# Expert tiles on GpSimd: the row store ahead of the next gather, the gather in the middle of the weight piece

## The reference

```python
x = x + tanh(g_xattn) * attention(layernorm(x), ctx, ctx, mask, W1, b1, W2, b2)
h = layernorm(x)
route = softmax(h @ router_w + router_b); e = argmax(route); p = max(route)
for each expert e:                       # w1[e]: 256 x 2048, w2[e]: 1024 x 256
    a, g = split(h @ w1[e], 2)
    y = (silu(a) * g) @ w2[e]            # kept for the tokens of e
x = x + tanh(g_ffn) * y * p
```

## Time and profile before

| | before |
|---|---|
| median of 3 runs | 448.74 us (445.57 to 452.37) |
| profiled execution, its own time | 449.49 us |
| its span, first to last instruction | 447.7 us |
| mean granted TensorE clock | 0.954 of 2.4 GHz |
| busy: PE, DVE, ACT, POOL | 401.3, 217.0, 176.5, 243.7 us |
| the loop over expert tiles | from about 107 us on |

### The profile page before, as it was taken

One profiled execution on the slowest core, in us unless ns is written; L12 is line 12 of the kernel. 1 busy time (PEld: TensorE's weight loads), 2 busy tenths in 40 slices (PEclk: granted clock), 3 DMA queues, 4 the chain that ended last, 5 costly groups with the idle time before them and its releaser, 6 DMA issues.

```text
span 447.7 us, 9834 instructions
## 1 busy us (share of the span) xinstructions
PE 401.3 (90%) x2431; PEld 346.5 (77%) x2432; DVE 217.0 (48%) x527; ACT 176.5 (39%) x338; POOL 243.7 (54%) x324
## 2 busy tenths in 40 slices
PE   5998984149989999999999999999999999999990
PEld 4787872027878888888888888888888888888880
DVE  4689899933454443444433444433444434444340
ACT  1167650024443454545532344445433543233230
POOL 2356997221865577887772258728852676232221
PEclk9999897559999999999999999999999999999996
DMA  7950233863333044333442003433331011000010
GB/s 204 360 199 2 95 107 131 85 175 108 118 118 117 23 166 163 135 117 116 134 155 83 27 17 117 134 112 124 117 117 35 4 35 35 24 24 27 24 33 12
DMA packets 29850, 44.01 MB, mean 98 GB/s; under 512 B 8377, under 2 KB 25581, under 8 KB 27791
## 3 DMA queue, kind: packets, MB, share of 16 engines
q1 hardware_dynamic: 24095, 34.45, 24.6%
q0 software_dynamic: 3456, 9.11, 6.3%
q10 hardware_dynamic: 2288, 0.33, 0.5%
HBM read 35.44 MB, written 8.83 MB: 99 GB/s over the span
## 4 chain that ended last, share of the span: by engine, by line
PE 80%; DVE 7%; POOL 6%; DMA 2%; issue 2%; ACT 1%; DVEq 0%; SPq 0%; POOLq 0%; ACTq 0%
PE py L1117 22%; PE pa L1099 21%; PE pg L1099 21%; PE ph L1109 7%; POOL w_lo L415 2%; PE px L1084 2%; DVE x_all L742 1%; PE ps_s L1024 1%; POOL rstd L399 1%; DMA ctx_in<-in_ctx 1%; DVE bn L750 1%; DMA x_sorted<-residual_rows,idx_gather 1%; PE ps_p L968 1%; PE ps_xt L940 1%; DVE x_norm L878 1%
## 5 line engine op out<-in xcount | busy, mean ns | idle before, releaser
L895 DVE TENSOR_TENSOR ht_lo<-ph,ht_hi 128x512 fp32r<-128x512 f32 x70 | 48.4, 691 | 135.4 <-ACT ht_hi L624 135.4
L493 POOL TENSOR_TENSOR w_lo<-staging,w_hi x84 | 107.1, 1304 | 7.3 <-ACT w_hi L645 4.0
L624 ACT CAST ht_hi<-ph 128x512 fp32r<-128x512 f32 x70 | 41.1, 586 | 118.6 <-PE ph L1109 83.4
L1117 PE MATMUL py<-w_hi,ht_hi 128*128 x280 | 81.3, 291 | 0.8 <-DVE out_tile L903 0.8
L1117 PE MATMUL py<-w_lo,ht_hi 128*128 x280 | 78.4, 280 | 0.0
L1117 PE MATMUL py<-w_hi,ht_lo 128*128 x280 | 78.3, 280 | 0.0
L482 POOL DMA_INDIRECT out<-out_tile,idx_now x34 | 34.6, 1019 | 72.6 <-DVE out_tile L903 72.0
L1099 PE MATMUL pa<-w_hi,xt_hi 128*128 (+1 forms) x140 | 58.7, 420 | 0.8 <-ACT xt_hi L606 0.8
L443 POOL DMA_INDIRECT x_sorted<-residual_rows,idx_now x34 | 35.6, 1048 | 39.5 <-DVE x_norm L878 21.4
L1099 PE MATMUL pg<-w_lo,xt_hi 128*128 (+1 forms) x140 | 55.9, 400 | 0.0
L1099 PE MATMUL pg<-w_hi,xt_hi 128*128 (+1 forms) x140 | 55.9, 399 | 0.0
(11 more groups left out here) (168 smaller groups left out, 583.2 us busy)
## 6 DMA issues: line engine op xcount, KB each, us to landing
staging<-in_L_ffn_w SPq DMA_DIRECT2D x24, 1024.0 KB
residual_rows<-x_all SPq DMA_DIRECT2D x8, 516.0 KB, 4.0
x_all<-in_x SPq DMA_DIRECT2D x8, 512.0 KB, 10.1
x_sorted<-residual_rows,idx_now POOLq DMA_INDIRECT x34
out<-out_tile,idx_now POOLq DMA_INDIRECT x34, 2.5
w_in<-in_L_xattn_W SPq DMA_DIRECT2D x2, 256.0 KB, 4.7
ctx_in<-in_ctx SPq DMA_DIRECT2D x1, 308.0 KB
mask_in<-in_fside_1xSxS ACTq DMA_DIRECT2D x1, 308.0 KB, 11.7
```

The lines of the kernel that those rows point to most:

```text
L493: lo = nc.gpsimd.tensor_tensor(out=w_lo[:, bass.ds(dst + q * QW, QW)], in0=staging[:, bass.ds(src + q * QW, QW)], in1=w_hi[:, bass.ds(dst ...
L624: nc.scalar.copy(ht_hi[:, j], ph[j][:]).then_inc(hhi_ready[j], 1)
L895: nc.vector.tensor_tensor(out=ht_lo[:, j], in0=ph[j][:], in1=ht_hi[:, j].bitcast(FP32), op=ALU.subtract).then_inc(hlo_ready[j], 1)
L1117: last = mm(py[:, 0:D], ht[:, j, c * P:(c + 1) * P], w[:, bass.ds(slot + (DC * PW + (j * HC + c) * D), D)], start=j == 0 and n == 0, stop= ...
```

## The change

In part 2 GpSimd's order within a tile becomes: load the piece number, index copies, store of tile t-1, quarters one and two of the weight piece, gather of tile t+2, quarters three and four. The piece's routine is cut into two halves, each in a branch of its own; in a tile without a piece both are skipped. The wait for `w_hi` stands ahead of the first half, the signal `w_ready` behind the last quarter, as before. The other engines' loops are not touched.

In part 1 the multiplication of round 0 by the token number moves from GpSimd to VectorE, where rounds 1 and 2 have it already, and the semaphore for it is gone.

```diff
-            end_group = ROUNDS[0][1]
-            pool.wait_ge(col_ready, 1)
-            nc.gpsimd.tensor_tensor(out=col_hot[:, 0:end_group], in0=col_hot[:, 0:end_group],
-                                    in1=token_of[:, 0:end_group].unsqueeze(2).to_broadcast([P, end_group, COLS, B]),
-                                    op=ALU.mult).then_inc(token_ready, 1)
...
-            def low_part(t):
-
-                piece = pool.value_load(tile_piece[:, bass.ds(t, 1)], min_val=0, max_val=E * PIECES - 1)
+            def low_half(piece, half):
+
                 with pool.If(piece > 0):
                     src = pool.snap((piece % PIECES) * PW)
                     dst = pool.snap(((piece // PIECES) & 1) * EW + src)
-                    pool.wait_ge(w_hi_ready, piece + (N_CHUNK - PIECES + 1))
-                    for q in range(QUARTERS):
+                    if half == 0:
+                        pool.wait_ge(w_hi_ready, piece + (N_CHUNK - PIECES + 1))
+                    for q in range(half * QUARTERS // 2, (half + 1) * QUARTERS // 2):
...
-                    lo.then_inc(w_ready, 1)
-
+                    if half == 1:
+                        lo.then_inc(w_ready, 1)
+
+            def piece_of(t):
+                return pool.value_load(tile_piece[:, bass.ds(t, 1)], min_val=0, max_val=E * PIECES - 1)
 
             def tile(t):
+                piece = piece_of(t)
                 index_copies(t)
+                scatter(t - 1, out_tile)
+                low_half(piece, 0)
                 pool.wait_ge(xnorm_ready, t + 2)
                 pool.wait_ge(res_ready, t + 2)
                 gather_rows(t + 2, idx_now[:, 0:1])
-                scatter(t - 1, out_tile)
-                low_part(t)
-
-            low_part(0)
+                low_half(piece, 1)
+
+            piece = piece_of(0)
+            low_half(piece, 0)
+            low_half(piece, 1)
             tile(1)
...
-                slots = nc.vector.tensor_tensor(out=slot_hot[:, at], in0=of_group(slot_iota, P),
-                                                in1=of_token(pos_f[:, 1], P), op=ALU.is_equal)
-                if r == 0:
-                    slots.then_inc(hot_ready, 1)
-                else:
-                    dve.wait_ge(col_ready, r + 1)
-                    nc.vector.tensor_tensor(out=col_hot[:, at], in0=col_hot[:, at], in1=of_token(token_v[:], COLS),
-                                            op=ALU.mult).then_inc(hot_ready, 1)
+                nc.vector.tensor_tensor(out=slot_hot[:, at], in0=of_group(slot_iota, P), in1=of_token(pos_f[:, 1], P),
+                                        op=ALU.is_equal)
+                dve.wait_ge(col_ready, r + 1)
+                nc.vector.tensor_tensor(out=col_hot[:, at], in0=col_hot[:, at], in1=of_token(token_v[:], COLS),
+                                        op=ALU.mult).then_inc(hot_ready, 1)
...
-                if r == 0:
-                    pe.wait_ge(token_ready, 1)
                 pe.wait_ge(hot_ready, r + 1)
```

More of the change, by code:

```diff
@@ L275, in flamingo_block @@
         col_ready = sem("col_ready")
-        token_ready = sem("token_ready")
         hot_ready = sem("hot_ready")
```

## The result

The changed kernel takes 561.86 us (median of 6 runs, 558.89 to 563.82), the kernel before in the same session 449.06 us (6 runs, 445.57 to 452.37): 1.250 times the time, 95% interval 1.246 to 1.254. The forecast was 546 us, so the loss is 113 us where 97 were forecast. The profiled execution of the changed kernel took 563.82 us.

A forecast was written before the change was run, and what follows sets the result against it. TensorE bounds the kernel before; after the change the ring does. Profiled 449.49 us + 71.4 for the loop - 0.6 for the sort = 520.3, with 26 for the clock 546 us; own range 528 to 575, wider range 512 to 576.

The forecast's parts named there:

- The ring: Expert loop, out_tile through store, half piece, gather and x_norm to out_tile: 12.91 us with a piece, 9.77 without.
- more in a tile that starts an expert: In six of 20 rings with a piece, the first quarter starts 1.43 and not 1.07 after the store: 2.2 us.
- The gather's setup: On GpSimd behind the second quarter: setup overlaps the running quarter, so the gather follows 0.05 us later; bounds 0 and 0.86.
- The lock on x_norm: VectorE's x_norm is held by GpSimd's quarters until 0.2 us after the fourth: 0.54 us per tile with a piece, 11 in all.
- the 0.15 us for the semaphore: Part of the 2.85 us taken for a gather travelling alone to land.
- The clock: TensorE idles 3.4 us in 20 tiles and falls to half clock in most: 1.3 us a tile, 26 us in all.
- the sort: Part 1, round 1: VectorE's indicator op shortens from 1.59 to 0.50 us; gain taken as 0.6 us.
- Full clock: Rival: late gather and all of the ring, but no clock falls in the loop; 520 us, chance 0.18.
- Setup not overlapping: Rival: gather's setup adds 0.81 us in each of 33 rings; 547 us at full clock, 573 with falls, chance 0.08.
- Gather beside a load: Rival: gather travels beside a weight load, 2.3 us more in 20 rings; 555 us without falls, 581 with, chance 0.05.
- Not slower: Rival: ring stays under TensorE's 9.52 us because rows reach x_norm in time; 447 us, chance 0.05.

The follow-up runs named there:

- warm kernel: Changed kernel plus 26 unread matmuls of 256 columns ahead of x_norm's transposes, in tiles whose predecessor carried a piece; 527.74 us, ratio 1.178.
- the kernel with the early load: Against the kernel before with only the multiplication moved to VectorE: piece number loaded at the tile's head, piece in one branch; 482.78 us, ratio 1.074.
- 13 matmuls: Changed kernel plus 13 unread matmuls of 256 columns ahead of x_norm's transposes, in tiles whose predecessor carried a piece; 534.8 us, ratio 1.191.
- the small copy: Changed kernel with the gather back ahead of the store, plus a 128x1 GpSimd copy between store and first quarter; 490.54 us, ratio 1.085.
- eight instructions: Changed kernel with the gather back ahead of the store, and the piece cut into eight instructions instead of four; 449.67 us, ratio 0.997.
- two halves: Changed kernel with the gather back ahead of the store, the two branches and the early piece-number load kept; 484.4 us, ratio 1.070.

## Why the prediction was right

**The ring** is the mechanism, as forecast. The length of it by steps, in the changed kernel against the prediction:

| step, in us | predicted | measured |
|---|---|---|
| out_tile's end to the store | 0.87 | 0.88 |
| store to first quarter, and two quarters | 3.62 | 3.61 |
| gap ahead of the gather, with a piece | 0.05 | 0.16 |
| gather's start to x_norm's end, with a piece | 3.85 | 3.72 |
| x_norm's end to out_tile's end, full clock | 4.52 | 4.50 |
| sum, with a piece | 12.91 | 12.87 |
| the same without a piece | 9.77 | 10.15 |
| more in a tile that starts an expert | 0.36 | 0.35 |
| x_norm's end to out_tile's end, more in a fall of the clock | 1.3 | 1.96 |

The store, the piece, the landing of the gather that travels alone, and the way back over px and `down` were all read off rows of the kernel before, and hold to 0.02 us but for the gather. One ring with a piece is 0.04 us shorter than forecast, which over 20 rings is 1 us. That it is so little is partly luck: the gap is 0.11 us longer than forecast, and gather's start to x_norm's end 0.13 shorter.

**The gather's setup** does overlap with the running quarters, so the rival with 0.81 us more in every ring fell: the gap is 0.16 us behind a quarter. Without a piece it is 0.31 us behind the store's record. The prediction had 0.04 there, as it let the gather follow after 1.07 like a quarter. These 13 rings took 132.0 us in place of 127.0: 3.5 us of it is that gap, the rest landings that came 0.3 to 0.8 us later in three of them. It is the second largest error.

**The lock on x_norm** holds: it ends 0.16 us behind the fourth quarter in 19 of 20 rings, and takes 0.72 us in the row above, not 0.41. It was worth less than the 0.54 us a tile taken for it. On the mean of the 20 rings x_norm starts 2.94 us after the gather's start (2.90 forecast; no row of the kernel before shows the 0.15 us for the semaphore in it) and takes 0.78, so the lock costs 0.37: the quarters end earlier than forecast, 3.56 after the gather's start and not 3.65.

The prediction misread how far this lock can reach. The Trainium skill, page "SBUF — State Buffer", section "Who interferes with whom", says of VectorE's instructions in two-port modes that the engine that issues first has the shared ports for its whole instruction while the other blocks. The prediction found the 1.98 us of the earlier trace rows in agreement with it. They go beyond it: that x_norm starts at 122.96 in the third quarter, the fourth starts at 123.48, and x_norm ends behind the fourth, at 124.94, so it was passed over at a boundary. The rows with 2.8 to 3.4 us in the experiments show more of the same: there VectorE is kept out at two boundaries, for the rest of one of GpSimd's instructions and two more, so the block lasts longer than the instruction that was running. In the changed kernel this made no difference, since the rows land in the last quarter. With the gather right behind the store it made all of it.

**The clock** is the term that was mis-sized, and the larger part of the error. The step read: "A fall of that length costs at most half of 3.4, or 1.7 us ... I take 1.3 a tile, 26 us in all". The falls came in every tile with a piece, 20 of 20, but seven of them lasted 6.8 us and lay over nearly all of px, ph and `down`: they began up to 1.1 us ahead of x_norm's end and ended 1.2 to 1.4 us ahead of out_tile's. By the rings, the way from x_norm to out_tile grew by 1.5 us in the thirteen short falls and by 2.75 in the seven long ones: 13 x 1.5 + 7 x 2.75 = 39 us. The warm kernel gives 38 by its rings and 34 by its median. The fall of the earlier trace rows was a short one, and one row was taken for the length of all, though the same trace has a stretch of 30.7 us at 1.2 GHz, from 71.7 to 102.4, in which TensorE is busy for 8.9 us. That the real figure lay within the bounds of 0 and 3.7 us a tile follows from those bounds being wide.

Together, in the profiled executions: forecast for the rings 387.4 + 26 = 413.4 us, measured 430.6. Of the 17.2 us between, 13 are the clock, 5 the tiles without a piece, and -1 those with one. The rest of the loss is -0.6 us ahead of the rings, as forecast for the sort, though profiled kernels with the same sort differ there by up to 7 us, and 0.2 us behind them.

**The rivals.** Full clock (520 us): refuted by 20 falls, and borne out as a sum by the warm kernel: 520.3 and the 5 us for the tiles without a piece make 525.3, where its profiled execution took 526.6. The prediction names two ranges, 528 to 575 and 512 to 576; 561.9 lies in both, but only the second leaves room for this rival. Setup not overlapping: refuted by the gap of 0.16. Gather beside a load: refuted in this kernel by x_norm's end at 3.72. Not slower: refuted, though the run with the gather a tile further ahead is that rival's condition met by another edit, and it takes 450 us.

**What the prediction did not see** is that the change had a second cost lying ready. With the gather early as before, the mere load of the piece number at the tile's head costs 33 us, as x_norm is then held until the end of the piece. In the changed kernel that doesn't come on top, since its ring waits until the end of the piece anyway.

## What to carry to other kernels

Before moving a transfer behind a store, look for the ring: if what the transfer feeds must be done before the next store of the same kind can go, the time from store to store is the sum of the chain, whatever the engines' busy shares say. Ask then for how many turns ahead the transfer is; one tile more of it turned 562 us into 450 at the same order. And when a chain leaves TensorE idle for some microseconds in every turn, price the clock with both ends: the matmuls behind the gap are in the chain, at half speed.

## What the runs showed of the hardware that was not expected

- VectorE's x_norm (0.41 us alone) can be kept out by back-to-back GpSimd instructions of 1.25 us over several boundaries: 2.8 us in the kernel with the early load, 2.8 to 3.4 with the gather right behind the store. Whether it gets in at the first boundary changed with one register load elsewhere in GpSimd's loop, which moved the quarters by 0.03 us, and was worth 33 us in all, 6 of them by the clock.
- Idle time of TensorE ahead of px and falls of the clock, in the tiles with a piece: after 3.0 to 3.6 us a fall in 20 of 20 (changed kernel, and again with the gather right behind the store), after 2.02 to 2.20 us in 14 of 20 (the kernels with 13 matmuls, with the small copy and with eight instructions), after 1.90 to 1.96 us in 9 of 26 (two halves, early load), after the one of 1.86 us, and after 1.55 to 1.80 us in none of 19. The falls last 3.4 or 6.8 us in the changed kernel, and up to 10.2 behind the idle times of 7.7 us and more of the kernel with the gather behind the piece. What decides between a fall and none, or between the lengths, is left open.
- A gather of 128 rows has x_norm done 3.2 to 3.4 us after its start when it is alone, in ten of 13 tiles (3.7 to 4.1 in the others), and after 5.4 to 6.3 us when a 1 MB load has been released just ahead of it.
